# Loading the first expert weights by number into space that attention has left, and products of constants in TensorE's waits, in a fused two-layer transformer kernel

## The reference

```python
# layer 0: h = layernorm(x)*(1+ca)+sa; x = x + ga*attention(h)   16 heads of 128, causal softmax
#          h = layernorm(x)*(1+cb)+sb; x = x + gb*(shared expert + 8 routed experts, top 2)
# layer 1: x = x + ga*linear_attention(layernorm(x)*(1+ca)+sa)
#          x = x + gb*ffn(layernorm(x)*(1+cb)+sb)
def _L1_ffn_ref(x, norm_w, gate_w, gate_b, w1, b1, w2, b2):
    t = xf * rsqrt(mean(xf * xf) + EPS) * norm_w
    vals, idx = top_k(t @ gate_w.T + gate_b, 4)
    G = zeros.at[rows, idx].set(softmax(vals))
    h = einsum('mh,eoh->emo', t, w1) + b1
    a = minimum(h[..., ::2], 7); b = clip(h[..., 1::2], -7, 7)
    act = a * sigmoid(1.702 * a) * (b + 1)
    y = einsum('emi,edi->emd', act, w2) + b2
    return x + einsum('me,emd->md', G, y)
```

## Time and profile before

| | us |
|---|---|
| median of 3 runs | 1042.82 |
| lowest and highest | 1041.34, 1048.06 |
| the profiled execution's own time | 1043.59 |
| its span, first to last instruction | 1041.7 |
| TensorE busy in the span | 970.5 (93%) |
| VectorE, ScalarE, GpSimd busy | 722.6, 671.3, 427.1 |

### The profile page before, as it was taken

The page is one execution under the profiler, slowest core; times in us unless marked ns, Lnnn a source line. Parts: engine busy times, 40 slices in busy tenths (PEclk is TensorE's granted clock), DMA queues, the critical chain, the costliest instruction groups (busy, mean ns, idle before and its releaser), DMA issues.

```text
span 1041.7 us, 20507 instructions
## 1 busy us (share of the span) xinstructions
PE 970.5 (93%) x6020; PEld 820.9 (79%) x6020; DVE 722.6 (69%) x2545; ACT 671.3 (64%) x1944; POOL 427.1 (41%) x450
## 2 busy tenths in 40 slices
PE   6999999999999999999999999996888799999990
PEld 4669888887988888888888888884677689999980
DVE  3564775777677678677867867776867668888870
ACT  2657786687677767757866776782735456676650
POOL 3322431342362353154236225224064555665673
PEclk9999999999999999999999999998999899999995
DMA  9928993994789210020012004057177699998954
GB/s 307 307 80 301 376 371 113 375 377 164 278 293 376 96 62 1 18 88 31 1 62 73 2 1 165 3 183 264 52 188 169 188 247 217 225 226 215 225 133 81
DMA packets 93725, 180.53 MB, mean 173 GB/s; under 512 B 9949, under 2 KB 29085, under 8 KB 92717
## 3 DMA queue, kind: packets, MB, share of 16 engines
q1 hardware_dynamic: 73467, 148.55, 43.1%
q0 software_dynamic: 18800, 30.30, 12.9%
q10 hardware_dynamic: 1346, 0.36, 0.2%
HBM read 77.71 MB, written 107.99 MB: 178 GB/s over the span
## 4 chain that ended last, share of the span: by engine, by line
PE 86%; DVE 4%; issue 3%; ACT 2%; DMA 2%; POOL 1%; SPq 0%; ACTq 0%; DVEq 0%; POOLq 0%; another core or an unknown queue 0%
PE bank L1076 12%; PE bank L1040 11%; PE bank L1012 10%; PE bank L1085 6%; PE bank L1030 5%; PE bank L1002 5%; PE bank L991 4%; PE bank L962 3%; PE bank L868 3%; PE bank L1031 3%; PE bank L1001 3%; PE bank L1021 3%; PE bank L877 3%; PE bank L946 2%; PE bank L984 2%
## 5 line engine op out<-in xcount | busy, mean ns | idle before, releaser
L1076 PE MATMUL bank<-RB 128*128 128x128 f32 x1264 | 157.8, 279 | 6.1 <-issue 3.8
L1076 PEld LDWEIGHTS bank<-RB 128*128 128x128 f32 x1264 | 150.6, 195 | 9.6 <-issue 4.6
L1871 POOL TENSOR_TENSOR RB<-RB 128x512 f32<-128x512 f32 x64 | 67.6, 1056 | 203.1 <-DVE RB L1650 203.1
L1040 PE MATMUL bank<-RA,RB 128*128 128x256 f32 x512 | 133.7, 383 | 1.1 <-DVE X L1690 0.8
L1341 ACT ACTIVATE RB<-RA,nw 128x512 f32 x158 | 105.5, 715 | 37.2 <-issue 16.5
L1012 PE MATMUL bank<-RA 128*128 128x256 f32 x512 | 121.2, 380 | 0.0
L1012 PEld LDWEIGHTS bank<-RA 128*128 128x128 f32 x512 | 95.2, 190 | 15.0 <-issue 2.9
L1040 PEld LDWEIGHTS bank<-RA,RB 128*128 128x128 f32 x512 | 91.0, 190 | 15.5 <-issue 4.7
L1847 POOL TENSOR_TENSOR qs<-qs,half 128x4 f32<-128x4 f32 x64 | 64.9, 1014 | 93.1 <-DVE qs L1659 79.6
L1085 PE MATMUL bank<-RB,BC 128*128 128x256 f32 x316 | 83.2, 387 | 3.3 <-DVE BC L1777 2.3
L1242 ACT ACTIVATE RB<-bank 128x256 f32<-128x256 f32 x128 | 48.7, 381 | 57.9 <-PE bank L1031 52.8
(11 more groups left out here) (251 smaller groups left out, 2387.3 us busy)
## 6 DMA issues: line engine op xcount, KB each, us to landing
xsD<-BC SPq DMA_DIRECT2D x17, 4232.0 KB, 33.0
RB<-in_w2b SPq DMA_DIRECT2D x79, 256.0 KB
...
RA<-in_w SPq DMA_DIRECT2D x2, 2048.0 KB, 8.0
RA<-in_w SPq DMA_DIRECT2D x6, 512.0 KB, 11.5
RA<-in_L_attn_Wq SPq DMA_DIRECT2D x1, 2048.0 KB, 13.8
```

The lines of the kernel that those rows point to most:

```text
L1040: m = pe.matmul(bank[5][:, t * 256:t * 256 + 256], OT[:, u % 2, t * 128:t * 128 + 128], Wo[:, h, :], start=(h == 0 and t == 0), stop=(h == ...
L1076: m = pe.matmul(ps[:, 128 * j:128 * j + 128], WS[:, n % 2, c, 128 * j:128 * j + 128], XT[:, n % 2, c * 128:c * 128 + 128], start=(c == 0), ...
L1871: pool.tensor_tensor(sq, qrow, qrow, ALU.mult).then_inc(mine("q_sq", p), 1)
```

## The change

Three things are done, and the planner's numbers are changed with them.

- **Weights by number.** `w12(0)` is gone. `w1x(n)` for the blocks n = 0 to 3 reads the expert's number from the table and loads the weights of that expert into place 4, 5, 10 or 12 of W1. `h_mm(n)` reads them there, unscaled, with no `w_in(n)`; norm_w is put on the tokens, by `x_out(n)` in two halves. When `h_mm(n)` is done, `w12x(n)` loads expert 4, 5, 10 or 12 into its place. `w_in(4)` and all later ones wait for `w12x(3)` too.
- **Products of constants.** `keep_busy` goes through TensorE's list behind `wo(127)`. Where the planner has a wait ahead of a step that takes a new bank, it puts `idle(n)`: n products of the identity and ones in bf16, 128x128, into that bank (22 places, 81 products). At the program's start TensorE does nine 128x512 products of ones in bf16, after VectorE has filled P[:,0,:].
- **The planner.** FIRST is 22. `KV, SHARED, LINEAR, FILL, TURN` go from 0.04, 0.02, 0.06, 0.19, -0.09 to -0.08, 0.07, -0.02, 0.24, 0.11. The chains of elements 5, 6 and 7 behind attention get an allowance: while `wo(127)` is not planned none, afterwards 1 for element 5.

```diff
+PLACES = 4, 5, 10, 12
+DURING, BEHIND = {5: 0, 6: 0}, {5: 1, 6: 0, 7: 0}
+    def keep_busy(self, since):
+        order, at = [], None
+        for k in self.order:
+            if k in self.end and self.engine({"do": k}) == "PE":
+                begin = self.end[k] - ENGINE[k[0]][1]
+                if at is not None and self.end[since] <= at and k in self.turn:
+                    n = min(12, int((begin - at - 0.3) / 0.16))
+                    if n > 0:
+                        order.append(("idle", n, *k))
...
-        yield do("h_mm", n, ..., after=[("w_in", n)] + ...)
+        yield do("h_mm", n, ..., after=[("w1x", n), ("wo", NU - 1)] * (n < len(PLACES)) + [("w_in", n)] * (n >= len(PLACES)) + ...)
...
+            def w1x(n):
+                on.wait_ge(*done("n_bi", 0))
+                on.wait_ge(*done("pv", NU - 17))
...
+                r = sp.value_load(table(0, n), min_val=0, max_val=15)
+                sp.dma_start(W1[:, PLACES[n]:PLACES[n] + 1, :, :]..., I["w1"]...[:, bass.ds(r, 1), :]...).then_inc(mine("w1x", n), 16)
+            def w12x(n):
+                on.wait_ge(*done("h_mm", n))
+                e = PLACES[n]
+                sp.dma_start(W1[:, e:e + 1, :, :]..., I["w1"][:, 1024 * e:1024 * e + 1024]).then_inc(mine("w12x", n), 16)
...
+            def idle(n, *stage):
+                on.wait_ge(L["cb16"], 32)
+                clear(*stage)
+                for _ in range(n):
+                    pe.matmul(psum(*stage)[:, 0:128], identb, ones_b, start=True, stop=True)
+            on.wait_ge(awake, 1)
+            for _ in range(9):
+                pe.matmul(bank[1][:, :], ones_w[:, 0:128], ones_w[:, 128:640], start=True, stop=True)
...
                 on.wait_ge(*done("w12", 2))
+                on.wait_ge(*done("w12x", len(PLACES) - 1))
```

More of the change, by code:

```diff
@@ L59 @@
 }
-HOP, LANDING = 0.2, {"bc": 5.0, "mod_store": 4.0, "clear": 14.0, "w12": 11.0, "xb": 3.2, "w2x": 3.5, "y_add": 4.0, "f_send": 3.0, "store": 4.0}
+HOP, LANDING = 0.2, {"w1x": 5.0, "w12x": 6.0, "bc": 5.0, "mod_store": 4.0, "clear": 14.0, "w12": 11.0, "xb": 3.2, "w2x": 3.5, "y_add": 4.0, "f_send": 3.0, "store": 4.0}
 LANDED = {"x0": 4.5, "cT": 4.0, "wmA": 6.0, "wk": 10.0, "wv": 11.5, "wq": 17.0, "wo": 24.0, "x": 30.0, "wmB": 45.0, "wm1": 50.0, "sw": 55.0, "small1": 55.0, "tables": 20.0, "w0": 60.0}
@@ L111, in add, with chain, allowance @@
         self.order.append(k)
-    def chain(self, late, steps):
-        self.chains.append([late, steps, next(steps), 0.0])
+    def chain(self, late, steps, of=None):
+        self.chains.append([late, steps, next(steps), 0.0, of])
+    def allowance(self, c):
+        late, of = c[2].get("late", c[0]), c[4]
+        return late + (BEHIND if ("wo", NU - 1) in self.end else DURING).get(of, 0.0)
     def begin(self, c):
-        late, steps, ask, ready = c
+        late, steps, ask, ready, _ = c
         t = ready
@@ L173, in run @@
                 self.chains.remove(c)
+    def keep_busy(self, since):
[7 more added lines that the diff above has]
+                        order.append(("idle", n, *k))
+                at = self.end[k]
+            order.append(k)
+        self.order = order
 def do(stage, *key, **how):
@@ L419, in last_weights @@
     def last_weights():
-        yield do("w12", 0, by=48, aside=True, after=[("pv", NU - 17), ("k_mm", NB - 1, 1), ("v_mm", NB - 1, 0), ("v_mm", NB - 1, 1)])
         yield do("w12", 1, by=32, aside=True, after=[("q_mm", NU // 2 - 1)])
@@ L432, in block @@
         yield do("x_out", n, bank=1, last=True, late=TURN, after=[("h_mm", n - 2)] * (n >= 2))
-        yield do("h_mm", n, bank=2 + n % 2, first=True, after=[("w_in", n)] + [("h_mm", n - 1)] * (n > 0))
+        yield do("h_mm", n, bank=2 + n % 2, first=True, after=[("w1x", n), ("wo", NU - 1)] * (n < len(PLACES)) + [("w_in", n)] * (n >= len(PLACES)) + [("h_mm", n - 1)] * (n > 0))
         yield do("e_a", n, bank=2 + n % 2, after=[("res", 0, NB - 1), ("s_x", NB - 3, 1)] * (n == 0) + [("e_act", n - 2)] * (n >= 2) + [("e_b", n - 1)] * (n > 0))
@@ L449, in weights_in, with first_weights, weights_behind @@
     def weights_in():
-        for n in range(FIRST):
-            yield do("w_in", n, aside=True, after=[("w12", 2), ("n_bi", 0)] + [("h_mm", n - 2)] * (n >= 2))
+        for n in range(len(PLACES), FIRST):
+            yield do("w_in", n, aside=True, after=[("w12", 2), ("w12x", len(PLACES) - 1), ("n_bi", 0)] + [("h_mm", n - 2)] * (n >= len(PLACES) + 2))
+    def first_weights():
+        for n in range(len(PLACES)):
+            yield do("w1x", n, slot=n, by=16, aside=True, after=[("n_bi", 0), ("pv", NU - 17), ("k_mm", NB - 1, 1), ("v_mm", NB - 1, 0), ("v_mm", NB - 1, 1)])
+    def weights_behind():
+        for n in range(len(PLACES)):
+            yield do("w12x", n, by=16, aside=True, after=[("h_mm", n)])
     def weights_out():
@@ L466, in lay_out @@
     p.chain(LATE, last_weights())
-    for steps in (weights_in(), weights_out(), block(0)):
+    for steps in (first_weights(), weights_behind(), weights_in(), weights_out(), block(0)):
         p.chain(FILL, steps)
     p.run()
+    p.keep_busy(("wo", NU - 1))
     lo, hi, ahead = FIRST, NBLK, 8
@@ L834, in _ @@
             run = {"mod_store": mod_store, "bc": bc, "acc_zero": acc_zero, "zrow_store": zrow_store,
-                   "clear": clear, "xb": xb, "w12": w12, "w2x": w2x, "store": store}
+                   "clear": clear, "xb": xb, "w1x": w1x, "w12x": w12x, "w12": w12, "w2x": w2x, "store": store}
             for stage, *key in plan.order:
@@ L1070, in h_mm @@
                 ps = psum("h_mm", n)
-                on.wait_ge(*done("w_in", n))
+                if n < len(PLACES):
+                    w = W1[:, PLACES[n], :, :]
+                    on.wait_ge(*done("w1x", n))
+                else:
+                    w = WS[:, n % 2, :, :]
+                    on.wait_ge(*done("w_in", n))
                 on.wait_ge(*done("x_out", n))
@@ L1347, in x_out @@
                     on.wait_ge(*done("h_mm", n - 2))
[L1348 removed]
+                if n < len(PLACES):
+                    on.wait_ge(L["small1"], 128)
+                    for c in range(2):
+                        m = act.activation(XT[:, n % 2, 128 * c:128 * c + 128], psum("x_out", n)[:, 128 * c:128 * c + 128], ACT.Copy, scale=nw[:, c:c + 1])
+                    m.then_inc(mine("x_out", n), 1)
+                else:
+                    act.activation(XT[:, n % 2, :], psum("x_out", n)[:, 0:256], ACT.Copy).then_inc(mine("x_out", n), 1)
             def e_tanh(n):
```

44 lines of the change are left out of this document (23 added, 21 removed), and 2 rows, old and new, of the table ENGINE.

## The result

| | before, us | after, us |
|---|---|---|
| median | 1045.22 (20 runs, 1040.64 to 1048.06) | 1047.78 (20 runs, 1044.94 to 1054.38) |
| ratio | | 1.0039, 95% interval [1.0026, 1.0053] |
| profiled execution, its span | 1043.59, 1041.7 | 1046.24, 1044.2 |

By the medians the change made the kernel slower by 2.6 us (the ratio is that of the means, 1044.8 and 1048.9), where I had forecast 1034.0, and 1047.78 lies above the top of my range. That is the first half of the result. The second half came from running the same two kernels again: on other occasions the changed kernel took 1032.52 us beside 1042.05, ratio 0.9917 [0.99, 0.9933], and 1029.38 beside 1040.17, ratio 0.9893 [0.9855, 0.9931]. What tells the occasions apart is in the trace.

A forecast was written before the change was run, and what follows sets the result against it. Bounds were TensorE's work in attention, then element 7's chain, then 2.87 us per block left. Terms -4.5 - 2 - 1 - 2.9, with 0.8 back for waits and code, gave -9.6: 1034.0 (own range 1030 to 1038; 8 in 10: 1024 to 1043).

The forecast's parts named there:

- T: The end of `wo(127)`, attention's last product, at 712.74 before; moved work was to bring it 4.5 us sooner.
- the start: Program's start: nine constant products raise TensorE's clock for the first products, -2 us, between 0 and -3.7.
- waits and code: Allowance of 0.8 us for waits that a new order may open in attention, and for code.
- Work moved behind T: End of attention: products go from ahead of `wo(127)` to behind it, so T comes 4.5 us sooner.
- The new wait: Behind T: `y_mm(0)` waits 2 us for the load `w2x(0)`; +1.8, `s_mm(7)` ending at T + 18.3.
- The router and the experts: Layer 0, element 7, behind T: router +2.7 us, experts +3, experts starting at T + 25, `d_y(7,1)` at T + 52.
- From there to `f_rank(1,7)`: From `d_y(7,1)` to `f_rank(1,7)`: 59.1 us becomes 51, -8, between -2 and -14, reaching T + 103.
- the better rival: TensorE becomes full: the later stretch falls to its work, 45 us, and the start gives 3.7; 1026, chance 23%.
- The constants: Behind attention: 81 constant products run in waits and cost 0 us, between -3 and +4.
- One more block: FIRST = 22: one block fewer in the loop, -2.9 us, while `f_rank(1,7)` to the second table's rows stays 27.1.
- The slower rival: Behind T: `w2x(0)`, the first `y_mm`'s weights, lands late and holds everything up; 2.6 us slower, 1046, chance 10%.

The follow-up runs named there:

- e11: The kernel before, unchanged, run again on an occasion with prompt signals: 1040.47 us (1 run).
- e9: The changed kernel, unaltered, run again on an occasion with prompt signals: 1032.52 us beside 1042.05 for the kernel before, ratio 0.9917.
- e17: The changed kernel with the load `w2x(0)` moved ahead of `w12(2)` in SyncE's list: 1049.44 us, ratio 1.0051 to the kernel before.
- e18: The changed kernel with FIRST = 21 instead of 22: 1046.75 us, ratio 1.0025 to the kernel before.
- A: Four runs with constants or planner taken out of the changed kernel, or put alone into the kernel before: ratios to before 0.9991 to 1.0144.
- F: Two runs of the changed kernel, one with `w2x(0)` loaded earlier, one with FIRST = 21: ratios to the kernel before 1.0051 and 1.0025.
- B to E: Runs with shortened sends, the changed kernel and the kernel before again, and parts of the change again: ratios to before 0.9865 to 1.0067.

## Why the prediction was wrong

It was wrong on the occasions with late signals, as that of the result was, and I had no term for them: neither the forecast nor a rival has a wait on TensorE's signals in it. On the others the total was right. The spans of e11 and e9 are 1038.6 and 1029.0, -9.6, as forecast; 1032.52 is inside my own range, and 1029.38 just under it, inside the range for 8 in 10. That the total is met to 0.1 us is luck, for the parts are not:

| part, prompt signals (e11, e9) | forecast | measured |
|---|---|---|
| T, with the start | -6.5 | -4.5 |
| T to `f_rank(1,7)` | -1 | -4.9 |
| from there to the second table's transposes | 0 | +2.6 |
| from there to the last `h_mm` | -2.9 | -4.0 |
| the end, and waits and code in the forecast | +0.8 | +1.2 |
| sum | -9.6 | -9.6 |

- *Work moved behind T (-4.5) and the start (-2).* **The step that failed is "attention is bound by TensorE's work, so T comes 4.5 sooner".** With late signals T is 0.7 later. I had read 596.6 of 600 as proof that nothing else mattered. What I take for the cause, though no run shows it by itself, is that the cover of the last units' chain was the work that I counted as moved, and the sends of element 5 moved into that place. The earlier trace rows showed no sign of it; the order showed the sends' new place, and I only counted their bytes. With prompt signals T is 4.5 sooner (710.77 to 706.25), which is the moved work. The start gave nothing: without constants T is the same (704.73 for the start of `wo(127)` against 705.22 and 704.9). The timeline of after shows where my 2 went:

```profile
6.27 1.92 PE L960 MATMUL bank<-sT,BC 128*128 128x8 f32 x16 [1.00 <-DMA BC<-in_L_wmod]
...
9.89 3.78 PE L913 MATMUL bank<-RA 128*128 128x512 f32 x4 [1.11 <-ACT RA L1255]
13.46 2.79 PE L922 MATMUL bank<-RA 128*128 128x512 f32 x4
...
17.80 1.89 PE L1070 MATMUL bank<-RA 128*128 128x256 f32 x8
```

`modc_mm` takes 1.92 for 3.55, but behind it the clock is back at 0.50 from 8.5 to 15.3, `k_mm` takes 3.78 for 3.54 and `v_mm` 2.79 for 1.88. `q_mm(0)` starts 0.8 sooner (17.80 against 18.59), and nothing of that is left at T.
- *The new wait, +1.8.* It is there, 2.46 and 2.41, and `s_mm(7)` takes 2.59 for 4.16. It ends at T + 20.1, not T + 18.3, but in e17 it ended at T + 15.9 and the experts still began later, so this end alone decides nothing.
- *The router and the experts.* The experts' first product is at T + 23.0, not T + 25, and `d_y(7,1)` at T + 52.2, as forecast at T + 52.
- *From there to `f_rank(1,7)`.* T + 98.9 against T + 103: from `d_y(7,1)` at 765.64 it took 46.7, not my 51, so it gave 12 and not 8. That is near the 45 of the better rival, TensorE's own work.
- *The constants, 0.* Right: 0.9906 without and 0.9917 with them. The constants' clock gave nothing that reaches the end.
- *One more block, -2.9, with 27.1 kept.* **The second step that failed.** The loop is 3.5 to 4.0 shorter, but the stretch ahead of it is longer: +2.6 with prompt signals, +8.9 with late ones. The 22nd block by itself puts 3.4 on it (e18 against after), so the 27.1 held TensorE's work and its handshakes too, not GpSimd's and SyncE's chain alone.

The slower rival (1046) gave nearly the time, but not by its mechanism: `w2x(0)` landed at T + 12.2 and held up little.

**What stays open:** why TensorE's signals are late in the bursts on some occasions, and what in the bursts does it. Three of the seven occasions had them (that of the result, A and F), one chip had both kinds, and the queue that GpSimd feeds shows no more time for its packets with late signals than without. The page's row of that queue, of after:

```profile
q0 software_dynamic: 18800, 30.30, 12.8%
```

In e9 it has the same packets and MB with 13.1% of a shorter span, so 134 us in after (12.8% of 1044.2) and 135 in e9 (13.1% of 1029.0).

Two things went along with the late signals, and either may be the cause. Groups A and F ran their kernels in five rounds, B to E in three. And the eight traces with late signals lack records: they hold 1213 to 1229 raisings of TensorE's semaphores and 4889 to 5193 raisings by DMAs, the twelve others 1278 to 1280 and 6310 to 6401. So the recording of the profile may have a part in holding the signals back. Every run here has a recorded span and clock, so none tells what these kernels take without a recording.
